# Talking-heads top-k attention on one core: VectorE's step turned, one pass moved to GpSimd

## The reference, cut to what matters

```python
# x is (16, 512, 128): 16 batches. 16 heads of width 64, 16 memory keys, top 64 of each row are kept.
x = x + layernorm(attn(layernorm(x)))
x = x + layernorm(ffn(layernorm(x)))          # silu-gated, width 384

def attn(x):
    q, k, v = heads(x @ Wq), cat(mem_k, heads(x @ Wk)), cat(mem_v, heads(x @ Wv))
    dots = einsum('bhid,bhjd->bhij', q, k) * scale
    dots = einsum('bhij,hk->bkij', dots, pre_proj)      # heads are mixed before the softmax
    dots = where(causal, neg, dots)
    vk = top_k(dots, 64)[0][..., -1:]                   # the 64th largest score of each row
    dots = where(dots < vk, neg, dots)
    attn = softmax(dots)
    attn = einsum('bhij,hk->bkij', attn, post_proj)     # and mixed again after it
    return merge(einsum('bhij,bhjd->bhid', attn, v)) @ Wo + bo
```

## Time and profile before

| what | value |
|---|---|
| median of 3 runs | 3636.49 us (3635.76 to 3638.41) |
| profiled execution, its own time | 3636.07 us |
| its span, first to last instruction | 3634.3 us |
| mean granted clock of TensorE | 0.884 of full |
| busy: VectorE, ScalarE, GpSimd | 3292.4, 3199.3, 1551.4 us |
| busy: TensorE matmul, weight load | 2795.9, 1808.7 us |

### The profile page before, as it was taken

The page is one execution under the profiler, slowest core; times in us unless marked ns, Lnnn a source line. Parts: engine busy times, 40 slices in busy tenths (PEclk is TensorE's granted clock), DMA queues, the critical chain, the costliest instruction groups (busy, mean ns, idle before and its releaser), DMA issues. The chain is left out here.

```text
span 3634.3 us, 67348 instructions
## 1 busy us (share of the span) xinstructions
PE 2795.9 (77%) x13751; PEld 1808.7 (50%) x13751; DVE 3292.4 (91%) x12492; ACT 3199.3 (88%) x9018; POOL 1551.4 (43%) x2663
## 2 busy tenths in 40 slices
PE   7777778777777878778778867877777788877765
PEld 3455455545545545555455545544555455545544
DVE  4699999999999999999999999999999999999994
ACT  1799999999979999999999979998999999999973
POOL 3233444444434444444444444443444444444433
PEclk9888999988888899888998888899889998899886
DMA  1000000000000000000000000000000000000000
GB/s 41 7 2 2 5 8 5 8 2 5 8 4 8 5 8 2 5 8 5 8 5 7 2 4 8 5 8 2 5 8 5 8 5 8 2 5 8 2 7 4
DMA packets 31375, 22.37 MB, mean 6 GB/s; under 512 B 3201, under 2 KB 30338, under 8 KB 30722
## 3 DMA queue, kind: packets, MB, share of 16 engines
q1 hardware_dynamic: 30722, 16.03, 1.6%
HBM read 11.83 MB, written 4.19 MB: 4 GB/s over the span
## 5 line engine op out<-in xcount | busy, mean ns | idle before, releaser
L871 ACT ACTIVATE signs<-scores,state 128x528 int8<-128x528 f32 (+3 forms) x3072 | 1764.3, 574 | 181.8 <-DVE state L1149 103.4
L713 PE MATMUL s_bank<-xn,gT 128*128 128x512 f32 (+3 forms) x2048 | 900.6, 568 | 1.7 <-issue 0.7
L1269 POOL TENSOR_SCALAR probs<-probs,rinv 128x528 f32<-128x528 f32 (+3 forms) x1024 | 547.1, 553 | 507.3 <-DVE rinv L1053 507.3
L737 PE MATMUL t_bank<-ident,probs 128*128 128x128 f32 x2560 | 482.7, 313 | 299.1 <-POOL probs L1269 289.7
L724 PEld LDWEIGHTS y_bank<-u_all,probsT 128*128 128x128 f32 x5120 | 619.9, 194 | 133.4 <-issue 124.2
L724 PE MATMUL y_bank<-u_all,probsT 128*128 128x128 f32 x5120 | 625.2, 278 | 7.1 <-ACT probsT L882 7.1
L1260 POOL TENSOR_TENSOR offset<-consts,found 128x36 f32<-128x36 f32 x256 | 161.7, 632 | 1047.5 <-DVE work L1014 1047.5
L871 ACT ACTIVATION_READ_ACCUMULATOR signs<-scores,state 128x1 f32 x3072 | 575.7, 187 | 0.0
L737 PEld LDWEIGHTS t_bank<-ident,probs 128*128 128x128 f32 x2560 | 299.7, 153 | 506.8 <-issue 398.6
L1048 DVE SCALAR_TENSOR_TENSOR probs<-scores,kth,expo 128x528 f32<-128x528 f32 (+3 forms) x1024 | 522.8, 565 | 24.8 <-issue 19.1
L892 ACT ACTIVATE expo<-scores,negmax 128x528 f32<-128x528 f32 (+3 forms) x1024 | 535.0, 575 | 0.0
(11 more groups left out here) (148 smaller groups left out, 3384.9 us busy)
## 6 DMA issues: line engine op xcount, KB each, us to landing
xwork<-in_L_attn_x_dram SPq DMA_DIRECT2D x17, 256.0 KB, 2.8
xres<-in_L_attn_x_dram SPq DMA_DIRECT2D x16, 256.0 KB, 2.9
out_dram<-ybuf SPq DMA_DIRECT2D x16, 256.0 KB, 2.4
u_all<-in_L_attn_Wq_dram SPq DMA_DIRECT2D x1, 512.0 KB, 3.7
u_all<-in_L_attn_Wk_dram SPq DMA_DIRECT2D x1, 512.0 KB, 4.5
u_all<-in_L_attn_Wv_dram SPq DMA_DIRECT2D x1, 512.0 KB, 5.3
u_all<-in_L_attn_Wo_dram SPq DMA_DIRECT2D x1, 512.0 KB
expo<-in_L_ffn_w_gate_dram SPq DMA_DIRECT2D x1, 192.0 KB, 4.7
```

What stands on the lines that cost most here:

```text
L713: nc.tensor.matmul(score_part(t, 0, KEYS[t]), lhsT=gT[s % 2][:, t * P:(t + 1) * P], rhs=xn[par][:, 0:KEYS[t]], start=True, stop=False, ski ...
L737: mm = nc.tensor.transpose(t_bank[q % 2][:, at:at + P], probs[:, h % 2, KEY_AT[t] + j * P:KEY_AT[t] + (j + 1) * P], ident[:, :])
L871: nc.scalar.activation(signs[:, k, 0:ROW[t]], row(scores, ring(head_of(s, k + 1), RING), t), ACT.Sign, bias=guesses(s % STATES, k, GUESSES ...
L1269: nc.gpsimd.tensor_scalar(prb, prb, rinv[:, slot_p, t:t + 1], 1.0, ALU.mult, ALU.mult).then_inc(scaled, 1)
```

## The change

- The pass of line 1080 leaves VectorE. GpSimd makes it as four two-input passes, one for each row tile (`scores - work`), behind the four normalising passes in its step; each waits for its own exact count and increments a new semaphore `hidden`.
- For a subtraction of 1 to push a score below all others, the scores carry a factor of 2^-60 (`UNIT`): it goes into the folded weights, the guess table, the mask, the bias of the exponential and its `scale`.
- VectorE's step is turned: scan and pick of the head that was counted one step earlier, masked product, reciprocal, exact count, `spread` and `missed`, eviction, the step's other work (layer-norm statistics, memory maxima, the feed-forward's product), and the update last. The flag's register is read between the second and the third scan.
- On GpSimd the copy of the memory scores comes ahead of the normalising, the rank offsets (line 1260) behind the new passes.
- TensorE sums the flag behind the first turn instead of the second; ScalarE takes it ahead of the exponentials instead of behind them.
- Some values and the `DOWN` products change their step in `EXTRAS`; the last layer norm moves from step 14 to 15, and the feed-forward's product on VectorE stands one step later.

```diff
+UNIT = 2.0 ** -60
+MASKED = -2.0 ** 40
# EXTRAS: 4 has one value fewer, U 8 to 15 shift, DOWN goes from step 13 to 14
# TensorE, step
                         turn(head_of(s, LAG_P), g - LAG_P, 0)
-                        turn(head_of(s, LAG_P), g - LAG_P, 1)
                     if flagged(kind, s):
...
+                        turn(head_of(s, LAG_P), g - LAG_P, 1)
                         turn(head_of(s, LAG_P), g - LAG_P, 2)
# ScalarE, step
                     take_turned(0)
+                    if flagged(kind, s):
+                        at_least(act, probs_ready, 4 * (g - LAG_K))
+                        take(kind, b, par, ("FLAG", s), flags[:, :], ...)
                     exponentials(0)
...
-                                                 bias=negmax[...]
+                                                 bias=negmax[...],
+                                                 scale=1.0 / UNIT
# VectorE, start of the step
+                    if applies:
+                        dve.wait_ge(hidden, 4 * gp + 4)
+                        alone(dve)
+                        for p, t in enumerate(ORDER):
+                            if p == 2:
+                                dve.wait_ge(misc_free, flag_index(kind, b, s) + 1)
+                                alone(dve)
+                                rows_missed = dve.value_load(...)
+                            v.max(candidates(past)[:, t, 1:9], work[...]).then_inc(select_step, 1)
+                        dve.wait_ge(offset_ready, gp + 1)
+                        dve.wait_ge(select_step, T + 1)
+                        v.scalar_tensor_tensor(out=offset[...], ..., in1=candidates(past), ...)
+                        dve.wait_ge(select_step, T + 2)
+                        v.tensor_reduce(kth[...], offset[:, :, :], AX_X, ALU.add).then_inc(kth_ready, 1)
# (masked product and reciprocal as before), then
+                    if selects:
...
+                        for t in ORDER:
+                            v.tensor_scalar(work[...], row(scores, slot_k, t), guessed[:, t:t + 1],
+                                            None, ALU.is_ge, ALU.add, accum_out=found[...]).then_inc(found_ready, 1)
+                        dve.wait_ge(found_ready, 4 * gk + 4)
+                        v.scalar_tensor_tensor(out=spread[:, :], ...).then_inc(select_step, 1)
+                        dve.wait_ge(select_step, 1)
+                        v.scalar_tensor_tensor(out=missed[:, 0:T], ...).then_inc(bad_ready, 1)
# (eviction, the step's other work, update)
-                        v.scalar_tensor_tensor(out=work[:, :], in0=work[:, :], scalar=-FMAX,
-                                               in1=scores[...], op0=ALU.mult, op1=ALU.add).then_inc(select_step, 1)
# GpSimd, step: behind the four normalising passes
+                    if lagged(kind, s, LAG_K):
+                        for p, t in enumerate(ORDER):
+                            pool.wait_ge(found_ready, 4 * gk + p + 1)
+                            alone(pool)
+                            wrk = work[:, AT[t]:AT[t] + ROW[t]]
+                            nc.gpsimd.tensor_tensor(wrk, row(scores, slot_k, t), wrk, ALU.subtract).then_inc(hidden, 1)
+                        at_least(pool, kth_ready, gk)
+                        alone(pool)
+                        nc.gpsimd.tensor_tensor(offset[:, :, 0:9], ranks, found[...], ALU.add).then_inc(offset_ready, 1)
```

More of the change, by code:

```diff
@@ L908, in step @@
                     take_turned(0)
+                    if flagged(kind, s):
+                        at_least(act, probs_ready, 4 * (g - LAG_K))
+                        take(kind, b, par, ("FLAG", s), flags[:, :], misc[misc_place(kind, par, ("FLAG", s))][0:1, 0:T + 1])
                     exponentials(0)
@@ L966, in _ @@
             dve.wait_ge(a_taken, 4)
[L967 removed]
+            nc.vector.scalar_tensor_tensor(out=a_sq[:, :, :], in0=a_all[:, :, :], scalar=1.0 / UNIT, in1=a_all[:, :, :],
+                                           op0=ALU.mult, op1=ALU.mult).then_inc(squared, 1)
             dve.wait_ge(squared, 1)
@@ L1053, in step @@
                         v.reciprocal(rinv[:, slot_p % 2, :], rowsum[:, :]).then_inc(rinv_ready, 1)
+                    if selects:
+                        guessed = guesses(now, GUESSES, 1)
+                        dve.wait_ge(guess_ready, g - 1)
+                        dve.wait_ge(mem_placed, gk + 1)
+                        dve.wait_ge(masked, 4 * gk + 4)
+                        alone(dve)
+                        for t in ORDER:
+                            v.tensor_scalar(work[:, AT[t]:AT[t] + ROW[t]], row(scores, slot_k, t), guessed[:, t:t + 1],
+                                            None, ALU.is_ge, ALU.add, accum_out=found[:, t:t + 1]).then_inc(found_ready, 1)
+                        dve.wait_ge(found_ready, 4 * gk + 4)
+                        v.scalar_tensor_tensor(out=spread[:, :], in0=found[:, :], scalar=-2.0 * AIM, in1=found[:, :],
+                                               op0=ALU.add, op1=ALU.mult).then_inc(select_step, 1)
+                        dve.wait_ge(select_step, 1)
+                        v.scalar_tensor_tensor(out=missed[:, 0:T], in0=spread[:, :], scalar=WINDOW ** 2 + 0.5 - AIM ** 2,
+                                               in1=active, op0=ALU.is_gt, op1=ALU.mult,
+                                               accum_out=missed[:, T:T + 1]).then_inc(bad_ready, 1)
                     if kind != "drain":
@@ L1063, in step @@
                                             accum_out=rowmax[:, bass.ds(slot, 1), t]).then_inc(masked, 1)
+                    if s == 0 and kind in ("first", "mid"):
+                        dve.wait_ge(x_in, 16 * (b + 2))
+                        norm_stats(kind, b, "x", xwork)
+                    if s == 8 and kind in ("first", "mid"):
+                        memory_maxima(kind, b, 1 - par)
                     if s == 6 and kind != "first":
@@ L1071, in step @@
                         norm_stats(kind, b, "X1", xres)
-                    if s == 14 and kind != "first":
+                    if 11 <= s < 11 + HC and kind != "first":
+                        c = s - 11
+                        dve.wait_ge(silu_pool, HC * (b - 1) + c + 1)
+                        v.scalar_tensor_tensor(out=f_up[:, c, :], in0=f_tanh[:, c, :], scalar=1.0,
+                                               in1=f_up[:, c, :], op0=ALU.add, op1=ALU.mult).then_inc(silu_ready, 1)
+                    if s == 15 and kind != "first":
@@ L1286, in step @@
                                               head_mem(smem[par], s)).then_inc(mem_placed, 1)
+                    gp, slot_p = g - LAG_P, head_of(s, LAG_P) % 2
+                    if lagged(kind, s, LAG_P):
+                        pool.wait_ge(rinv_ready, gp + 1)
+                        at_least(pool, probs_ready, 4 * gp + 4)
+                        alone(pool)
+                        for t in SCORE_ORDER:
+                            prb = probs[:, slot_p, AT[t]:AT[t] + ROW[t]]
+                            nc.gpsimd.tensor_scalar(prb, prb, rinv[:, slot_p, t:t + 1], 1.0, ALU.mult,
+                                                    ALU.mult).then_inc(scaled, 1)
+                    if lagged(kind, s, LAG_K):
+                        gk, slot_k = g - LAG_K, ring(head_of(s, LAG_K), RING)
+                        for p, t in enumerate(ORDER):
[4 more added lines that the diff above has]
+                        at_least(pool, kth_ready, gk)
+                        alone(pool)
+                        nc.gpsimd.tensor_tensor(offset[:, :, 0:9], ranks, found[:, :].unsqueeze(2).to_broadcast([P, T, 9]),
+                                                ALU.add).then_inc(offset_ready, 1)
+                    if lagged(kind, s, LAG_P):
+                        if s == LAG_P and kind != "first":
+                            pool.wait_ge(misc_full, misc_index(kind, b, ("PM", 1)) + 1)
+                        pool.wait_ge(scaled, 4 * gp + 4)
+                        alone(pool)
+                        nc.gpsimd.tensor_copy(head_mem(pmem, head_of(s, LAG_P)), mem_parts(probs[:, slot_p, :])).then_inc(pmem_ready, 1)
                     extras(kind, b, s)
```

126 lines of the change are left out of this document (26 added, 100 removed).

## The result

The changed kernel takes 3766.8 us (median of 4 runs, 3763.45 to 3768.74) against 3637.2 for the kernel before (now the median of 4 too): the ratio is 1.0356, with a 95% interval of 1.0338 to 1.0373. The forecast was 3595, faster by 41 us, with a range up to 3695. The time moved the other way, by 130 us, half a microsecond in each of the 256 steps.

What follows compares the result with a forecast made beforehand. VectorE was taken as the bound, ScalarE close behind. 16 x 0.02 + 2.4 = 2.7 us a batch, 43 in 16 batches less 2 at the end: 41 off 3636, so 3595 us; own range 3555 to 3628, whole range 3490 to 3695.

Steps and rivals of the forecast that it cites:

- What bounds it: Whole kernel: VectorE leads, busy 201.35 of 212.80 us a batch, with ScalarE close behind at 198.97.
- The floor of 3489: Time if ScalarE becomes the bound: 3636 - 147 = 3489 us, with coupling some 3500; chance 0.22.
- The port: GpSimd and VectorE hinder each other where both read two tensors; 1.65 us of stalls expected in a plain step.
- plain steps: Steps with nothing between eviction and update; 12.41 us before the change, eight of a batch's 16.
- the slower rival: GpSimd's port time paid in full in the update's chain, from 1.67 us of stall a step; some 3690 us, chance 0.27.
- T+2.35: Forecast end of spread, which waits for the normalising; T is the start of the exact count, right behind the reciprocal.
- The turned plain step: VectorE's reordered step: 4.66 us up to the exact count plus 7.73 to the update's end, 12.39 against 12.41.
- The other eight steps: Steps with work between eviction and update: stall shrinks from 0.4 to 0.1, 0.3 us won in each, 2.4 a batch.
- Moves at no cost: Reordered scan, rank offsets, flag matmul and copy, normalising and EXTRAS: claimed to cost nothing.
- the scan's slack: VectorE's scan waits for GpSimd's last pass: ready at T+5.9, wanted at T+7.7, 1.8 us in hand.

Runs made afterwards that it cites:

- no_passes: The changed kernel without GpSimd's four passes, the scan reading the scores instead of work (other values picked); 3476.6 us, ratio 0.9559.
- turn_only: The changed kernel's turned step, but with the pushing-down pass kept on VectorE between spread and missed and none on GpSimd; 3758.6 us, ratio 1.0335.
- no_branch: The changed kernel without the branch on missed rows and the general search in it, the flag still read; 3576.2 us, ratio 0.9836.
- turn_branch: Turned step with the pass on VectorE, and the branch on missed rows moved from behind the pick to behind the last scan; 3704.7 us, ratio 1.0199.
- branch_early: The changed kernel with the branch on missed rows moved from between pick and masked product to behind the last scan; 3730.1 us, ratio 1.0257.

## Why the prediction was wrong

**What bounds it** was right: VectorE before and after, with ScalarE close. The floor of 3489 was some 12 us too high: no_passes reached 3476.6, and there ScalarE still waited 35 us for the update.

**The port** was right in mechanism, and in size as a sum. Forecast: four passes of 3.6 us behind the normalising, `missed` held for 1.25 us, the update for 0.4 in plain steps and 0.1 in others: 1.5 on average. Measured against turn_only: 1.47, of which `missed` has 0.99, the update 0.31 and `spread`, for which the forecast had nothing new, 0.14. That the sum fits so well is in part luck. What I called "the slower rival", more than 1.67 us of stall, did not come. The prediction's "1.67 us taken off" and "1.65 of stalls" are not the sums of its own parts: it lets `spread` keep its wait, to T+2.35, so 1.55 us go (1.46 and 0.09) and 1.53 are lost. The difference, 0.02 us, is the same.

**The failed step is "The turned plain step"**: "Before it stand scan 1.84, pick 0.60, masked product 2.08, reciprocal 0.14: T is 4.66 us". I moved the pieces with the lengths that they had in the old order, start to start, and such a length belongs to an order. The pick's 0.60 was measured with the exact count behind it, which waited for nothing of the pick. With the masked product behind it, VectorE must finish the pick, wait for it and then take the branch with an empty engine. The table has it: pick to next 0.26 to 1.05 and reciprocal to next 0.14 to 0.24, 0.89 us a step or 228 us. In the old place the branch had two counts queued before it. no_branch puts 0.61 of the 0.79 us on the branch. The 0.18 that it leaves are the wait for the pick's own result and two waits more than the count has; no run parts them. The 0.10 behind the reciprocal are no wait for its result, which the count does not read: the count has three waits and a nop ahead of it, the eviction one wait.

In sum, a step was to be 0.17 us shorter and was 0.47 longer. The pass and its stalls (pass, `spread`, `missed`, update) were the whole forecast, -0.17, and came to -0.44: `missed` lost 1.00 and not 1.25, and the update grew by 0.07 and not by 0.25, as in the turned order it meets less of GpSimd's other work (1.91 in turn_only for 2.15 before). The waits and the branch, which I had at nothing, came to +0.89, the scan and the rest to some hundredths.

**The other eight steps** did better than the plain ones, as I said: from one update's end to the next the median of the plain steps 3 to 5 went from 12.45 to 13.05 us, 0.60 longer, and the mean step only 0.47. With the time of the moved statistics taken out, these eight steps lost 0.29 us each and the other eight 0.58; I had 0.3 between them.

**Moves at no cost**: the scan's slack, the offsets and the flag's new place held; of the flag's new place the waits say (after)

```profile
ACT flags L805 <- PE misc L762: 21.8, 28, 1.7
```

which is 21.8 us in all. What should have stood there is the branch: I wrote what is behind each moved instruction on the other engines, and not what was in front of the branch on its own.

The Trainium skill gives a price for it: Advanced Engine Details and Errata, "Control Flow Timing", has about 108 ns for compare-and-branch. Here the branch with nothing queued cost 0.61 us a step and under queued counts 0.15, so the figure is not what the engine loses, as far as these runs show.

## What to carry to other kernels

A start-to-start time taken from a trace is good only for the neighbours it was measured with: before an instruction is moved, ask what its new follower waits for and what the sequencer has to do between them, branches above all. Leave queued work in front of a branch, and look at every step after moving one: here the earlier place gave 0.43 us in plain steps and took most of it back in others. A wait put between two short instructions is paid as well (0.14 us here). Work moved to GpSimd that reads two tensors is paid on VectorE except as far as one-input work (here scan and eviction; the count was seen beside one-input work of GpSimd only) stands beside it: size the part that is moved to that cover, 528 columns of 1344 here, and not to the engine's idle share.

## What the runs showed of the hardware

- A conditional branch on VectorE's list whose body is skipped costs 0.6 us from pick to masked product with nothing queued in front of it (1.05 to 0.44) and 0.15 us a step with two passes queued (13.33 to 13.18). Behind queued scans it cost little in most steps, but gaps of 0.7 to 2 us came up in others (22 in turn_branch), each ending 1.7 to 2.0 us after the start of an 8 KB packet of the instruction queue.
- An instruction that waits for the result of the one just before it on its own engine starts later than one that does not: `spread` behind the last count against the eviction behind it, 0.12 us (2.06 and 1.94 us for the whole count); from pick to masked product 0.18 us, with two more waits in it.
- One more semaphore wait with its nop between two instructions that follow each other closely cost 0.14 us: from the update's last instruction to the first scan 0.10 us in the changed kernel, 0.24 in branch_early.
- GpSimd's subtraction of two tensors took 1298, 1034, 765 and 491 ns for 528, 400, 272 and 144 columns, 3.46 us for the four in a row; a two-input instruction of VectorE waits for the one in progress, and is served ahead of the next (0.46, 0.81 and 0.52 us beside the back-to-back passes of branch_early). The largest and the smallest, in the view grouped by shape of after:

```profile
L1261 POOL TENSOR_TENSOR work<-scores,work 128x528 f32<-128x528 f32 x256 | 332.2, 1298 | 0.6 <-DVE work L1069 0.6
...
L1261 POOL TENSOR_TENSOR work<-scores,work 128x144 f32<-128x144 f32 x256 | 125.7, 491 | 0.0
```
